# Two mixture-of-experts stages: who forms the remainders of the activations, who copies the kept results, and how the experts' matrices are loaded

## The reference

```
scores = softmax(layernorm(x) @ router_w.T)              # 8 experts
gate_vals, sel_idx = top_k(swapaxes(scores, 1, 2), 257)  # per batch and expert, over 1024 tokens
h = gelu(tokens @ w1[e] + b1[e])                         # 128 -> 512
y = h @ w2[e] + b2[e]                                    # 512 -> 128
out = zeros_like(x).at[b_idx, sel_idx].add(y * gate_vals)
```

## Time and profile before

| engine | busy us | share of span | instructions |
|---|---|---|---|
| TensorE matmul | 1003.5 | 86% | 5564 |
| TensorE weight load | 671.1 | 57% | 5564 |
| VectorE | 816.2 | 70% | 1285 |
| ScalarE | 682.5 | 58% | 1135 |
| GpSimd | 448.5 | 38% | 584 |

### The profile page before, as it was taken

How to read it: one execution, slowest core, us unless ns; L and a number is a source line. 1 busy time by engine, 2 the same in 40 slices (tenths; PEclk the granted TensorE clock), 3 DMA queues, 4 the chain that set the end, 5 groups by cost and what they waited for, 6 DMA issues and landing times. The chain is left out here.

```text
span 1171.9 us, 15732 instructions
## 1 busy us (share of the span) xinstructions
PE 1003.5 (86%) x5564; PEld 671.1 (57%) x5564; DVE 816.2 (70%) x1285; ACT 682.5 (58%) x1135; POOL 448.5 (38%) x584
## 2 busy tenths in 40 slices
PE   1848999999997889999966699999999778999897
PEld 0325555555545666777744355555555356677776
DVE  5537667677734788699973567766766278877996
ACT  0313566666664677677732166666666647766775
POOL 4013324442223365466526022222222316656563
PEclk9966999999998799999987599999999959999999
DMA  3394121121004000244106312121100130003421
GB/s 82 82 248 91 38 47 36 29 55 28 2 1 123 22 1 1 58 107 93 34 1 164 70 28 29 28 29 29 29 2 1 37 108 1 1 24 101 102 65 36
DMA packets 63629, 60.42 MB, mean 52 GB/s; under 512 B 5656, under 2 KB 56768, under 8 KB 62784
## 3 DMA queue, kind: packets, MB, share of 16 engines
q1 hardware_dynamic: 61328, 58.22, 21.8%
q10 hardware_dynamic: 2224, 1.20, 0.5%
HBM read 44.85 MB, written 14.29 MB: 50 GB/s over the span
## 5 line engine op out<-in xcount | busy, mean ns | idle before, releaser
L1016 POOL TENSOR_TENSOR f_hr<-f_h,f_hr 128x1024 fp32r<-128x1024 f32 x64 | 176.9, 2765 | 204.4 <-ACT f_hr L1185 204.4
L1179 ACT ACTIVATE f_h<-f_banks,b_t 128x512 f32<-128x512 f32 x256 | 166.7, 683 | 102.9 <-PE f_banks L1100 55.5
L1117 PE MATMUL f_banks<-f_hr,f_w2r 128*128 128x512 f32 x768 | 196.5, 402 | 14.3 <-DVE f_hr L1229 11.7
L1100 PE MATMUL f_banks<-f_xr,f_w1r 128*128 128x512 f32 x768 | 197.3, 403 | 0.0
L1117 PEld LDWEIGHTS f_banks<-f_hr,f_w2r 128*128 128x128 f32 x768 | 142.2, 191 | 48.3 <-issue 14.4
L830 DVE TENSOR_REDUCE b_mlate<-b_banks 128x2 f32<-128x1024 f32 (+3 forms) x120 | 124.7, 1079 | 60.0 <-PE b_banks L698 44.6
L830 DVE TENSOR_REDUCE a_mlate<-a_banks 128x2 f32<-128x1024 f32 (+3 forms) x120 | 124.7, 1079 | 59.7 <-PE a_banks L698 43.8
L1100 PEld LDWEIGHTS f_banks<-f_xr,f_w1r 128*128 128x128 f32 x768 | 145.9, 194 | 29.9
L1185 ACT ACTIVATE f_hr<-f_h 128x1024 fp32r<-128x1024 f32 x128 | 135.8, 1061 | 4.1
L690 PE MATMUL a_banks<-a_k,a_q 120*128 120x512 f32 (+3 forms) x384 | 107.3, 385 | 24.2 <-POOL a_k L646 10.9
L733 PE MATMUL b_banks<-b_q,b_k 121*128 121x512 f32 (+3 forms) x384 | 115.8, 384 | 10.3 <-DMA b_q<-b_mt 9.2
(11 more groups left out here) (215 smaller groups left out, 1349.9 us busy)
## 6 DMA issues: line engine op xcount, KB each, us to landing
f_w<-in_w SPq DMA_DIRECT2D x32, 256.0 KB, 3.6
v<-scratch_gate SPq DMA_DIRECT2D x32, 256.0 KB, 4.8
xt<-scratch_gate SPq DMA_DIRECT2D x32, 256.0 KB, 4.8
scratch_q<-a_q_hl SPq DMA_DIRECT2D x24, 128.0 KB, 3.1
scratch_k<-a_k_hl SPq DMA_DIRECT2D x24, 128.0 KB, 3.1
a_k<-scratch_k SPq DMA_DIRECT2D x8, 384.0 KB
a_q<-scratch_q SPq DMA_DIRECT2D x8, 384.0 KB
scratch_q<-b_q_hl SPq DMA_DIRECT2D x24, 128.0 KB, 5.3
```

Of the source, the lines that this page charges most:

```text
L1016: pool.tensor_tensor(hr[q % 2][1][:, 2:4, :], h[:, 2:4, :], hr[q % 2][0][:, 2:4, :].bitcast(F32), ALU.subtract).then_inc(low_late, 1)
L1100: last = pe.matmul(h_ps[:, j, :], w1r[e % 2][wp][:, j * P:(j + 1) * P], xr[xp][:, chunk(c)], start=(i == 0), stop=(i == 2))
L1117: last = pe.matmul(y_ps[:, q % 2, :], w2r[e % 2][wp][:, j, :], hr[q % 2][hp][:, j, :], start=(j == 0 and i == 0), stop=(j == HB - 1 and i ...
L1179: act.activation(h[:, j, :], h_ps[:, j, :], ACT.Gelu, bias=m.b1_t[:, e * HB + j:e * HB + j + 1]).then_inc(gelu_done, 1)
```

## The change

The tables of events:

```
+PLAIN = KEEP * NCH + 2                      # 14 chunks
+def plain(q): return q < PLAIN
+def beside_step(u):
+    return u + (FIRST_COUNT - u) % COUNT_EVERY if u < TIES else u
 for q in range(CHUNKS):
-    (unit_of(q) + 5, 1, "low", q)
-    (unit_of(q) + 17, 2, "keep" if q < KEEP * NCH else "gate", q)
+    (beside_step(unit_of(q) + 5), 1, "low", (q, 0, 2))
+    (beside_step(unit_of(q) + (8 if plain(q) else 10)), 1, "low", (q, 2, 3 if plain(q) else 4))
+    (unit_of(q) + 17, 2, "gate", q) if q >= KEEP * NCH
+def load_events():
+    events = [(0, 0, "first", 0), (0, 1, "second", 0), (0, 2, "first", 1), (0, 3, "second", 1), (TIES, 4, "gates", 0)]
+    for e in range(2, NE):
+        events.append((unit_of((e - 1) * NCH) + 6, 5, "first", e))
+        events.append((unit_of((e - 1) * NCH) + 14, 6, "second", e))
+    at = [u for u, _, what, q in EVENTS if what == "gate"]
+    for n in range(CHUNKS):
+        events.append((TIES if n < NGS else at[n - NGS] + 1, 7, "spread", n))
+    return sorted(events, key=lambda event: event[0:2])
```

VectorE makes all remainders: `low` has two parts for each chunk. In the 14 plain chunks the second part is inner block 2 alone; the fourth inner block keeps its fp32 value (`h_last`) and its share of the result is one plain fp32 matmul. A `low` that falls in the search is put behind a search step:

```
 def output(q, j):
+    if (q, j) in LOW_DONE:
+        pe.wait_ge(h_low, LOW_DONE[q, j])        # three fp32r matmuls as before
+    else:
+        pe.wait_ge(gelu_done, (q + 1) * HB)
+        last = pe.matmul(y_ps[:, q % 2, :], w2_last[:, e, :], h_last[q % 2][:, :], start=False, stop=True)
```

ScalarE makes the high part of block 2 alone in a plain chunk, and copies the kept results (`keep` is gone from VectorE):

```
+            if 0 <= q - 1 < KEEP * NCH:
+                act.wait_ge(y_mm, q)
+                act.activation(ykeep[:, q - 1, :], y_ps[:, (q - 1) % 2, :], ACT.Copy).then_inc(kept, 1)
```

The matrices pass through a ring of two raw pairs. SyncE's queue walks `load_events()`; the load of expert e waits until GpSimd has split expert e - 2. GpSimd only splits matrices, expert after expert, each as soon as its pair has landed and its target is free. `w2_last` (the last 128 rows of every w2, 512 KB) is loaded between the pairs of experts 0 and 1:

```
+        def matrix(e, w):
+            if e >= 2:
+                sp.wait_ge(w_split, 2 * e - 3 + w)
+            ... dma_start(raw[e % 2][:, w, :], ...).then_inc(m.w_in[e % 2], 16)
 def gpsimd(pool):
+        for e in range(NE):
+            pool.wait_ge(m.w_in[e % 2], weights_in(e))
+            for w, to in enumerate((w1r, w2r)):
+                if e >= 2 and w == 0: pool.wait_ge(h_mm, (e - 1) * NCH * HB)
+                elif e >= 2: pool.wait_ge(y_mm, (e - 1) * NCH)
+                link(pool.tensor_copy(to[e % 2][:, 0, :], raw[e % 2][:, w, :]))
+                pool.tensor_tensor(to[e % 2][:, 1, :], ..., ALU.subtract).then_inc(w_split, 1)
```

More of the change, by code:

```diff
@@ L147, in vector_events @@
     for q in range(CHUNKS):
-        events.append((unit_of(q) + 5, 1, "low", q))
-        events.append((unit_of(q) + 17, 2, "keep" if q < KEEP * NCH else "gate", q))
-        if q < KEEP * NCH:
+        events.append((beside_step(unit_of(q) + 5), 1, "low", (q, 0, 2)))
+        events.append((beside_step(unit_of(q) + (8 if plain(q) else 10)), 1, "low", (q, 2, 3 if plain(q) else 4)))
+        if q >= KEEP * NCH:
+            events.append((unit_of(q) + 17, 2, "gate", q))
+        else:
             events.append((unit_of(q + KEEP * NCH + 3) + 11, 3, "gate", q))
@@ L158, in vector_events @@
         events.append((BIAS + c * BIAS_EVERY, 5, "bias", c))
-    return sorted(events)
+    return sorted(events, key=lambda event: event[0:2])
[7 more added lines that the diff above has]
+        events.append((TIES if n < NGS else at[n - NGS] + 1, 7, "spread", n))
+    return sorted(events, key=lambda event: event[0:2])
 EVENTS = vector_events()
 GATED = [q for _, _, what, q in EVENTS if what == "gate"]
+LOADS = load_events()
+LOWS = [q for _, _, what, q in EVENTS if what == "low"]
+LOW_DONE = {(q, j): n + 1 for n, (q, first, end) in enumerate(LOWS) for j in range(first, end)}
+HIGHS = [(q, j, j + 2) if j < 2 or not plain(q) else (q, 2, 3) for q in range(CHUNKS) for j in (0, 2)]
+HIGH_DONE = {(q, first): n + 1 for n, (q, first, end) in enumerate(HIGHS)}
 def ring_table():
@@ L967, in sync, with spread_gate @@
     def sync(sp):
-        for e in range(NE):
+        def matrix(e, w):
             if e >= 2:
[L970 to L977, removed]
+                sp.wait_ge(w_split, 2 * e - 3 + w)
+            if w == 0:
+                sp.dma_start(raw[e % 2][:, w, :], a["w1"][e, :, :]).then_inc(m.w_in[e % 2], 16)
+            else:
+                sp.dma_start(raw[e % 2][:, w, :].rearrange("p (j d) -> p j d", j=HB),
+                             a["w2"][e, :, :].rearrange("(j p) d -> p j d", p=P)).then_inc(m.w_in[e % 2], 16)
+        def spread_gate(n):
+            e, c = divmod(GATED[n], NCH)
             if n >= NGS:
@@ L984, in sync @@
                          ).then_inc(m.g_in[n % 2], 16)
+        for _, _, what, i in LOADS:
+            if what == "first":
+                matrix(i, 0)
+            elif what == "second":
+                matrix(i, 1)
+                if i == 0:
+                    sp.dma_start(w2_last[:, :, :], a["w2"][:, (HB - 1) * P:HB * P, :].rearrange("e p d -> p e d")
+                                 ).then_inc(m.w2_in, 16)
+            elif what == "gates":
+                sp.wait_ge(scored, 3)
+                sp.dma_start(m.scratch["gate"].rearrange("t e i -> (t e) i"), gate_rows[:, :]).then_inc(gates_out, 16)
+                sp.wait_ge(gates_out, 16)
+            else:
+                spread_gate(i)
         if last_layer:
@@ L1099, in hidden @@
             for i, (wp, xp) in enumerate(((0, 0), (0, 1), (1, 0))):
[L1100 removed]
+                last = pe.matmul(h_ps[:, j, :], w1r[e % 2][:, wp, j * P:(j + 1) * P], xr[xp][:, chunk(c)],
                                  start=(i == 0), stop=(i == 2))
@@ L1112, in output @@
                     pe.wait_ge(kept, q - 1)
[L1113 to L1118, removed]
+                if c == 0:
+                    pe.wait_ge(w_split, 2 * e + 2)
+                if q == 0:
+                    pe.wait_ge(m.w2_in, 16 * (k + 1))
+            if (q, j) in LOW_DONE:
+                pe.wait_ge(h_low, LOW_DONE[q, j])
+                for i, (wp, hp) in enumerate(((0, 0), (0, 1), (1, 0))):
+                    last = pe.matmul(y_ps[:, q % 2, :], w2r[e % 2][:, wp, j * P:(j + 1) * P], hr[q % 2][hp][:, j, :],
+                                     start=(j == 0 and i == 0), stop=(j == HB - 1 and i == 2))
+            else:
+                pe.wait_ge(gelu_done, (q + 1) * HB)
+                last = pe.matmul(y_ps[:, q % 2, :], w2_last[:, e, :], h_last[q % 2][:, :], start=False, stop=True)
             if j == HB - 1:
@@ L1225, in split, with low @@
                               ).then_inc(x_split, 1)
[L1227 to L1234, removed]
+        def low(q, first, end):
+            dve.wait_ge(h_high, HIGH_DONE[q, first])
+            dve.tensor_tensor(hr[q % 2][1][:, first:end, :], h[:, first:end, :], hr[q % 2][0][:, first:end, :].bitcast(F32),
+                              ALU.subtract).then_inc(h_low, 1)
         def gate(q):
@@ L1342, in vector @@
             elif what == "low":
-                low(i)
-            elif what == "keep":
-                keep(i)
+                low(*i)
             elif what == "gate":
```

67 lines of the change are left out of this document (29 added, 38 removed).

## The result

The changed kernel took 1178.3 us (median of 8 runs, 1174.83 to 1184.32); beside it on the same chip the kernel before took 1170.19 us (median of 8, 1167.95 to 1174.22). The ratio is 1.0066, with a 95% interval of 1.0044 to 1.0089: slower by 0.4 to 0.9%, some 8 us, small but clear of the noise. The profiled execution took 1179.7 us against the forecast's 1177.6; its span is 1177.8 us, 5.9 longer than before.

What follows compares the result with a forecast made beforehand. The prediction took TensorE, 86% busy, as the bound. Its terms summed to +1.95 us a stage, +3.9 for two: 1177.6 us for the profiled execution, 1175.6 for the median; range 1161 to 1187, leaving out 2 in 10.

Steps and rivals of the forecast that it cites:

- likeliest mechanism: Whole kernel: search relieved of GpSimd's hold, but expert 4's load late; +3.9 us for two stages, chance 0.48.
- no change: Whole kernel: a difference under 0.5% (5.9 us), which the measurement can't tell from none; chance 0.41.
- slower: Whole kernel: the changed kernel takes measurably longer than before; chance 0.39.
- before chunk 0: Stage start: GpSimd's split of expert 1 holds one normalising instruction of VectorE; +1.0 us a stage, bounds 0 and 3.8.
- chunks 0 and 1: First chunks: remainders now behind search steps 0 and 1 make outputs late; +2.05 us a stage, bounds 0 and 3.
- chunks 2 to 11: The search: without GpSimd's remainder, VectorE's L1309 is no longer held; -5.7 us a stage, bounds -7.5 and 0.
- chunks 12 to 15: Behind the search: expert 4's load, queued behind eight spreads, delays chunk 16; +4.8 us a stage, bounds -1.1 and +6.5.
- low clock in chunk 16: After the wait before chunk 16, TensorE runs at 1.2 GHz once; +1.7 us a stage, bounds 0 and 3.4.
- chunks 16 to 27, rest: Gating chunks: VectorE needs 5.41 us a chunk, splits cost TensorE 6.3 us; -3.2 us a stage, bounds -9.6 and +1.5.
- last chunk: Stage end: the last remainder waits in VectorE's list behind the gate of chunk 30; +1.3 us a stage.
- The slower rival: Chunks 16 to 27: VectorE becomes the bound, paying whole splits; over 75 us there, total 1185, chance 0.20.
- The load was not hidden: Before chunk 16: the rival had expert 4's load hidden, no wait or low clock; 15.2 us less, 1160.4, chance 0.20.

Runs made afterwards that it cites:

- e2: The changed kernel with GpSimd waiting for the first hidden block of chunk 0 before it splits expert 1: 1172.18 us, 1.0004 of before.
- e3: The changed kernel with chunk 0's two remainders ahead of search steps 0 and 1 instead of behind them: 1169.41 us, one run.
- e6: The changed kernel plus one unused GpSimd subtract of 128x1024, which reads SBUF, in each of chunks 0 to 11: 1192.02 us, one run.
- e7: The changed kernel plus one unused GpSimd memset of 128x2800, which only writes, in each of chunks 0 to 11: 1179.26 us, one run.
- e8: The changed kernel without the plain fp32 block, VectorE making the remainders of all four blocks in the search too: 1178.77 us, 1.0068 of before.
- e11: The changed kernel with early expert loads, late split of expert 1, first and last remainders moved ahead, and no plain fp32 block: 1136.78 us, 0.9697 of before.
- e9: The changed kernel with the kept results copied by VectorE again, one chunk later in its list: 1177.78 us, 1.0043 of before.
- e1: The changed kernel with expert 4's two loads ahead of the gates' write in SyncE's list, not behind the eight spreads: 1162.73 us, 0.992 of before.
- e12: e11 with one more SBUF tile of 128x2800 that no instruction touches, placed ahead of the last remainder tiles: 1140.69 us, 0.9732 of before.

## Why the prediction was right, and where its terms were not

The range held, and the sum was near: +3.9 us forecast, +5.9 in the span of the profiled execution, +8.1 between the medians (1178.3 where 1175.6 was forecast). The likeliest mechanism came as told, with its sign, but the chances put "no change" a little ahead of "slower". That the sum came out so near is partly luck: the terms that came out too low, by 4.8 / 6.7 us a stage, and those that came out too high, by 5.8 / 5.6, cancel. By the steps, for one stage:

| step | forecast | measured, 1st / 2nd stage |
|---|---|---|
| before chunk 0 | +1.0 | +2.0 / +3.0 |
| chunks 0 and 1 | +2.05 | +1.0 / +1.5 |
| chunks 2 to 11 | -5.7 | -6.0 / -6.0 |
| chunks 12 to 15 | +4.8 | +7.2 / +8.4 |
| low clock in chunk 16 | +1.7 | +2.1 / +1.8 |
| chunks 16 to 27, rest | -3.2 | -7.5 / -7.8 |
| chunks 28 to 30 | 0 | +1.0 / +1.0 |
| last chunk | +1.3 | +1.2 / +1.2 |
| sum | +1.95 | +1.0 / +3.1 |

The other 1.7 us lie in the attention layers, which the change doesn't touch.

*Before chunk 0.* Right in kind (e2), half the size or less. I took one hit on a four-element instruction, and that came (L1260, 1.10 us). But I counted the four L1262, which have one SBUF input of 128 x 128, among those that are not held. They took 2.44 us instead of 1.12 (3.77 in the second stage).

*Chunks 0 and 1.* The waits for output came (1.28 and 1.44 us), and e3 removed them with their cause. From step 0's count to chunk 2 the forecast had 6.9 us, the traces 6.59 in both stages, and before 4.84: +1.75, near the +2.05. The rest is no part of the mechanism: ahead of that count the changed kernel was 0.7 us shorter in the first stage (0.2 in the second), because its clock rose 4.3 us behind the start of chunk 0 instead of 5.9. The forecast had no term for that.

*The search.* The hold is shown by e6 and e7. That it was TensorE's loss is read from the waits: 6.1 us for the count before, none after, and the window is 6.0 us shorter. The average chunk was to be 6.0 us and is 6.0; e8 and e11 confirm the 0.18 us for the plain matmul, e9 that the copies cost nothing.

*Chunks 12 to 15.* The sum from chunk 12 was 6.0 to the gates, 20.9 to the second load, 4.2 landing, 2.0 for cast and subtract: 33.2. The rows give 6.2 (473.30 - 467.12), 21.6 (494.92), 5.8 (500.76) and 2.1 (502.86): 35.7. The mis-sized term is the landing. I took it shorter than the 6.7 us that four spreads need; the page's median over all of these loads is 5.2 us. The spreads themselves came 0.7 us later, in the second stage 1.9. e1 shows that the queue's order was the whole cause. TensorE's own work was 28.4, not 27.3 (27.28 without the plain block, e11), which moves nothing in this sum.

*Chunks 16 to 27.* The clearest miss: -7.5 where I had -3.2, and without it the kernel would be some 9 us slower still. VectorE's list, chunks 20 and 21:

```profile
530.14 1.22 DVE L1272 TENSOR_TENSOR f_hr<-f_h,f_hr 128x1024 fp32r<-128x1024 f32 x1
531.28 0.68 DVE L1286 TENSOR_TENSOR f_scaled<-f_ykeep,v 128x512 f32<-128x512 f32 x1
...
535.32 1.22 DVE L1272 TENSOR_TENSOR f_hr<-f_h,f_hr 128x1024 fp32r<-128x1024 f32 x1
```

The step failed in its price of VectorE's own work. A chunk is 535.32 - 530.14 = 5.18 us, not 5.41: the instruction behind a remainder starts 0.08 us before it ends, where I added a gap of 0.035. Over twelve chunks that is 2.8 us. And the results of chunks 12 to 15 are written straight into the total, without an addition; two of these fall in the stretch, 1.4 us. Together 4.2 us of VectorE's time, near the 4.3 / 4.6 missed; no run takes the two apart. The price of a split was nearly right: in this window VectorE's instructions exceed their unhindered durations by 6.1 us, and five of the six splits lie in it (expert 7's second falls in chunk 28), 1.2 us each against 1.27. VectorE has no wait from 516.0 us on, as told, but it does not set the pace all along: a chunk leaves it 0.26 us (5.44 - 5.18), so that its lag shrinks between splits. TensorE goes at its own 5.44 us in most chunks and loses 2.2 us where a split holds VectorE: chunk 19 takes 6.51, chunk 23 5.70, chunk 24 6.27. The forecast's 6.3 is mis-sized by that much. The slower rival needed over 75 us here and got 67.5 without the low clock. The whole-split price of that rival is not borne out.

*Chunks 28 to 30.* I had nothing there. Expert 7's split runs into chunk 28 and holds VectorE, whose remainder TensorE waits for:

```profile
572.16 1.07 POOL L1049 CAST f_w2r<-f_raw 128x512 fp32r<-128x512 f32 x1
...
573.32 2.15 POOL L1050 TENSOR_TENSOR f_w2r<-f_raw,f_w2r 128x512 fp32r<-128x512 f32 x1
...
577.34 1.65 PE L1148 MATMUL f_banks<-f_hr,f_w2r 128*128 128x512 f32 x6 [0.60 <-DVE f_hr L1272]
```

*The rivals.* The load was not hidden; e1 is that rival made true, and came to 1162.73 where 1160.4 was worked out.

## What to carry to other kernels

When loads move from the start of a stage into a queue that is walked in order, list what stands ahead of each of them; two loads behind eight paced transfers cost all that the better balance of engines had won, and the same loads ahead of them (e1) cost no wait at that place. Where GpSimd holds VectorE, as here, the instruction to move is the one that reads the SBUF (e6), not the one that only writes (e7); look at every small instruction of the other engine under its window. The work of an engine without slack is priced from start to start of its own rows, not by adding durations.

## What the runs showed of the hardware

An SBUF tile that nobody touches, and which only moves the tiles behind it, changed the pace of TensorE: 5.54 instead of 5.44 us for 24 matmuls (about 4 ns each), in e6, e7 and e12 alike, 3.9 us over the kernel between e11 and e12. The mechanism is open.

A tensor_scalar in fp32 with one SBUF input (128 x 128, scalars per partition) was held by GpSimd's cast and subtract, four of them for 1.3 us in the first stage and 2.65 in the second, though the neighbouring batch statistics were not (four in 0.87 us beside a subtract as without one). GpSimd is held as well: its cast of 0.61 us took 1.07 and its subtract of 1.26 took 2.15 beside VectorE's instructions at chunk 28.
